# Graph network on one core: padding edges get rows of their own behind the slots, and the scatter to the slots carries no bound

## The reference

```
h_proj = jnp.einsum('nd,rde->rne', h, relation_weight)      # 32 relations, 64 x 64 each
t_r = h_proj[etype, src]
h_r = h_proj[etype, dst]
att = jnp.sum(t_r * jnp.tanh(h_r + efeat), axis=-1)         # one number for each edge
att_exp = jnp.exp(att - seg_max[dst])                        # softmax over the edges of a destination
a = att_exp / denom[dst]
h_nb = jax.ops.segment_sum(h[src] * a[:, None], dst, num_segments=N)
out = leaky_relu((h + h_nb) @ res_w1.T) + leaky_relu(h * h_nb @ res_w2.T)
```

## Time and profile before

| | before |
|---|---|
| median of 3 runs | 4424.13 us |
| lowest, highest | 4401.28, 4436.07 us |
| span of the profiled execution | 4246.6 us, instructions 40658 |
| PE / PEld / DVE busy | 49% / 39% / 64% |
| ACT / POOL busy | 33% / 68% |
| DMA | 547.79 MB, mean 129 GB/s |
| granted TensorE clock, mean | 0.657 of full speed |

### The profile page before, as it was taken

The page is one execution under the profiler, slowest core; times in us unless marked ns, Lnnn a source line. Parts: engine busy times, 40 slices in busy tenths (PEclk is TensorE's granted clock), DMA queues, the critical chain, the costliest instruction groups (busy, mean ns, idle before and its releaser), DMA issues.

```text
span 4246.6 us, 40658 instructions
## 1 busy us (share of the span) xinstructions
PE 2075.1 (49%) x10767; PEld 1665.6 (39%) x10767; DVE 2732.3 (64%) x5225; ACT 1412.2 (33%) x2876; POOL 2876.9 (68%) x4049
## 2 busy tenths in 40 slices
PE   6729995565664222122200004543556787676563
PEld 2216663444443121121100003443545666665563
DVE  9947765888886899999933324673776445444442
ACT  0028873332332222222210002211212211887773
POOL 8878867888885888676067776666666400578787
PEclk9969996555555555555555557776776766666665
DMA  6668864444443555555332224324334411122121
GB/s 236 240 234 262 262 233 142 131 133 142 142 140 123 158 171 170 181 171 166 118 78 76 67 69 140 112 59 127 110 96 122 127 56 48 50 67 56 55 57 29
DMA packets 261685, 547.79 MB, mean 129 GB/s; under 512 B 107792, under 2 KB 119930, under 8 KB 261462
## 3 DMA queue, kind: packets, MB, share of 16 engines
q1 hardware_dynamic: 179702, 445.68, 32.1%
q0 software_dynamic: 81760, 99.52, 9.7%
HBM read 275.18 MB, written 273.83 MB: 129 GB/s over the span
## 4 chain that ended last, share of the span: by engine, by line
POOL 50%; issue 19%; DVE 13%; PE 11%; ACT 4%; DMA 3%; POOLq 0%; SPq 0%; DVEq 0%; ACTq 0%
POOL arena L1316 17%; POOL work L1316 14%; POOL result L1311 8%; POOL slot_rows L1311 8%; POOL pause L1324 3%; PE banks L1887 2%; PE banks L1767 2%; PE banks L1896 2%; DMA work<-slot_rows 2%; DVE arena L810 1%; DVE arena L818 1%; PE banks L1868 1%; DVE work L620 1%; DVE arena L614 1%; PE banks L1947 1%
## 5 line engine op out<-in xcount | busy, mean ns | idle before, releaser
L1311 POOL DMA_INDIRECT result<-work,outi x392 | 475.4, 1213 | 368.5 <-DVE work L1018 247.3
L1311 POOL DMA_INDIRECT slot_rows<-work,dsafe x392 | 390.5, 996 | 280.9 <-POOL pause L1329 184.6
L1316 POOL DMA_INDIRECT arena<-g_by_node_and_edge,m_idx x392 | 453.3, 1156 | 168.2 <-POOL pause L1324 105.7
L1316 POOL DMA_INDIRECT work<-in_x,dsafe x392 | 439.6, 1121 | 112.6 <-POOL pause L1324 104.9
L1316 POOL DMA_INDIRECT arena<-h_by_node_and_edge,m_idx x392 | 412.6, 1053 | 111.5 <-POOL pause L1324 59.9
L1759 PE MATMUL banks<-ident,work 128*128 128x128 f32 x392 | 100.5, 407 | 718.9 <-ACT arena L1468 646.2
L1316 POOL DMA_INDIRECT arena<-input_and_place_by_node,src_i x252 | 313.1, 1243 | 74.6 <-POOL pause L1324 73.7
L1759 PEld LDWEIGHTS banks<-ident,work 128*128 128x128 f32 x392 | 68.9, 213 | 742.4 <-issue 662.2
L1854 PE MATMUL banks<-ident,work 128*128 128x128 f32 x556 | 118.0, 353 | 347.2 <-DMA work<-slot_rows 278.5
L1887 PE MATMUL banks<-pos,ident 112*128 112x128 f32 (+3 forms) x784 | 191.7, 385 | 79.1 <-DVE spare L909 58.0
L1958 PE MATMUL banks<-work,ident 128*128 128x65 f32 x784 | 170.8, 413 | 118.9 <-ACT work L1683 118.9
(11 more groups left out here) (332 smaller groups left out, 6861.2 us busy)
## 6 DMA issues: line engine op xcount, KB each, us to landing
slot_rows<-work SPq DMA_DIRECT2D x64, 834.0 KB, 7.9
work<-slot_rows SPq DMA_DIRECT2D x139, 384.0 KB, 3.4
input_and_place_by_node<-arena SPq DMA_DIRECT2D x49, 528.0 KB, 3.0
g_by_node_and_edge<-arena SPq DMA_DIRECT2D x49, 512.0 KB
arena<-x_of_destination SPq DMA_DIRECT2D x56, 448.0 KB, 4.2
work<-g_by_node_and_edge SPq DMA_DIRECT2D x49, 512.0 KB, 4.4
h_by_node_and_edge<-work SPq DMA_DIRECT2D x49, 512.0 KB, 6.6
work<-h_by_node_and_edge SPq DMA_DIRECT2D x56, 448.0 KB, 4.0
```

Source lines behind the costliest of these rows:

```text
L1311: pool.indirect_dma_start(out=table[:, :], out_offset=bass.IndirectOffsetOnAxis(ap=idx, axis=0), in_=of, in_offset=None, bounds_check=boun ...
L1316: pool.indirect_dma_start(out=to, out_offset=None, in_=table[:, :], in_offset=bass.IndirectOffsetOnAxis(ap=idx, axis=0)).then_inc(signal, 16)
```

## The change

`slot_rows` gets KE = 392 more rows behind the 71,168 slots. `slots_found` has one more instruction per part, which takes the smaller of the row number and `P * KS + column`. For an edge that is the row number it had; for a padding edge it is a row behind the slots, one for each column. The reads of `slot_rows` and its zeroing are limited to the first 71,168 rows. The scatter to the slots no longer passes a bound. In the built program the bound is a register, which a register move sets ahead of every scatter; these 392 moves are gone, 396 are left for the other scatters. Where a scatter is paced, the wait for the pause stood on the register move, and it now stands on the DMA itself. The scatter of results keeps its bound.

```diff
-        slot_t = nc.dram_tensor("slot_rows", (P * KS, RW), F32).ap()
+        slot_t = nc.dram_tensor("slot_rows", (P * KS + KE, RW), F32).ap()
...
-                os.did(ts(slot_row[:, lo:hi], slot_row[:, lo:hi], float(t0), None, ALU.add))
+                os.do(ts(slot_row[:, lo:hi], slot_row[:, lo:hi], float(t0), None, ALU.add))
+                os.did(stt(out=slot_row[:, lo:hi], in0=tile_no[:, 0:hi - lo], scalar=float(P * KS + lo), in1=slot_row[:, lo:hi],
+                           op0=ALU.add, op1=ALU.min))
...
-            lanes = slot_t.rearrange("(l s) w -> l (s w)", l=P)
+            lanes = slot_t[0:P * KS, :].rearrange("(l s) w -> l (s w)", l=P)
...
-            slots = slot_t.rearrange("(l s) w -> l s w", l=P)
+            slots = slot_t[0:P * KS, :].rearrange("(l s) w -> l s w", l=P)
...
+            def scatter_all(table, idx, of, signal):
+                pool.indirect_dma_start(out=table[:, :], out_offset=bass.IndirectOffsetOnAxis(ap=idx, axis=0),
+                                        in_=of, in_offset=None).then_inc(signal, 16)
+
...
-            def scatter_slowly(table, idx, of, bound, signal):
-                scatter(table, idx, of, bound, signal)
+            def scatter_slowly(table, idx, of, signal):
+                scatter_all(table, idx, of, signal)
...
-                    (scatter_slowly if s > PART_STEPS[1] else scatter)(slot_t, slot_row[:, t:t + 1], perm[:, q, k, :],
-                                                                       P * KS - 1, c_sent[q])
+                    (scatter_slowly if s > PART_STEPS[1] else scatter_all)(slot_t, slot_row[:, t:t + 1], perm[:, q, k, :],
+                                                                           c_sent[q])
```

## The result

The changed kernel takes 4662.47 us (median of 4, 4640 to 4663) against 4430.1 us of the kernel before (median of 4, 4401 to 4448): ratio 1.0525, interval 1.0478 to 1.0572. Predicted were 4337 us, faster. It is slower by some 232 us.

A forecast was written before the change was run, and what follows sets the result against it. POOL alone was taken to bound the kernel from 2180 to about 3178 us, the scoring chain behind that. 102 + 4 - 12 - 6 - 1 = 87 us off the median 4424 gave 4337 us, range 4295 to about 4390.

The forecast's parts named there:

- Paced scatters, 1.88 to 1.36 us: POOL's slot scatters, steps 9 to 27: 0.52 us saved each, 102 us for the 196 of steps 9 to 22.
- rival 3: Paced scatters: the 0.78 us idle belongs to the scatter, not the register move; 4420 us, chance 0.10.
- Unpaced scatters, 4 us: 126 slot scatters of steps 0 to 8: 0.03 us saved each, 4 us, if the bound takes the difference.
- New transfers and new DVE work, nothing: 176 padding rows written: nothing; five more DVE instructions: 1.5 us, of which 1 us counts.
- Given back to the scoring, 18 us: POOL waits for scoring on DVE, which falls behind: 12 us in part 0, 6 in part 1.
- the 102 of the first term: Saving on POOL from 196 paced scatters of steps 9 to 22, at 0.52 us each: 102 us.
- waits for ACT of some 12 us in steps 13 to 15: Expected sign: POOL waits some 12 us for ACT's copy of the scan there, less in steps 18 to 20.
- Rival 1: Scoring is less stiff than assumed and nothing is given back to it; 4318 us, chance 0.15.
- What lies around the span isn't touched.: Profiled span 4246.6 to about 4160 us; the same microseconds taken off the median, 4424 to 4337.
- Rival 4: Slower: busier POOL holds up DVE's small scoring instructions, 7 us per step for 1%; 4468 us, chance 0.04.
- Rival 2: Scoring steps stretch by 2.4 us each as slot loads take longer; gain 44, 4380 us, chance 0.16.
- The tail: From the last scan to 3608 us: as long as before, some 240 us.

The follow-up runs named there:

- e9: Kernel before with its bound in one register set once, so no move ahead of each slot scatter: 4657.27 us, ratio 1.0541.
- e18: Kernel before, bound in a register set once, two pauses behind first-stage gathers and scatters and gathers of steps 9 to 27: 4302.89 us, 0.9745.
- e17: Kernel before, bound and moves kept, with two pauses behind gathers of the first stage and of steps 9 to 27: 4369.26 us, 0.9914.
- e2: Kernel before with only the longer table, its 392 more rows never written or read: 4424.97 us.
- e4: Changed kernel with longer table and padding rows, but a bound and its register move again on the slot scatter: 4434.72 us.
- e1_before_again: Kernel before, unchanged, profiled once more: 4439.72 us, profile span 4479.8 us.
- e15: Changed kernel with two pauses behind first-stage gathers and behind scatters and gathers of steps 9 to 27: 4318.62 us, 0.9721.

## Why the prediction was wrong

*Paced scatters, 1.88 to 1.36 us.* Right: 1.37, with 0.28 of idle. The reading of the move was right, and rival 3 fell. e9 shows it from the other side: with the bound kept and the moves gone, the scatters stand 1.38 us apart. e18 against e17 shows what such a saving is worth where nothing is late: 66 us for 0.35 us per scatter.

*Unpaced scatters, 4 us.* About right: steps 0 to 8 last 354.5 instead of 355.3 us.

*New transfers and new DVE work, nothing.* Right (e2, e4).

*Given back to the scoring, 18 us.* This is the step that failed. I took what DVE needs, 184 us for four steps, as a property of the scoring alone, and let POOL's steps shrink against it. The need depends on POOL's pace: with the scatters at 1.37 us a step takes 62.9 us, not the 46 of that budget. The term was not 18 us but some 320: the 102 of the first term, all of it, and the 218 that the stage got longer. My waits for ACT of some 12 us in steps 13 to 15 are 24 to 30 us for each of the steps 11 to 15, and go on behind them. Rival 1, nothing given back, is off in the same direction.

*"What lies around the span isn't touched."* Wrong as a reading, and so is the sentence beside the table of times that the 155 to 190 us lie around the instructions. Span and time of the profiled execution are within 2 us of each other in every run behind the prediction; the profile ahead of the prediction was an execution in which PE's hand-overs were on time (2 + 6 us late in sum, none by over 1 us), and the timed runs were not like it. The profile could not warn of a delay that it did not contain. The gap of some 177 us between its span and the median could, and I explained it away. A second warning lay in the kernel: pauses behind DMAs, which do nothing for the result, keep DMAs apart, and a change that shortens the distance works against them.

*Rival 4* had the sign. It asked for 7 us more per scoring step to be slower by 1%, and it was 15 us and 5%, so its 4468 us is far too little. Its mechanism is not the one either. It asked for longer DVE instructions, and the exclusive lock of the Trainium skill (SBUF — State Buffer, on the shared pair) would show as such. The scans take 2158 ns on the mean in both kernels and the small ones of L886 and L884 424 and 421 ns. No row here shows POOL holding DVE: DVE was called late, and so was ACT. *Rival 2* named steps that stretch, by slot loads that take longer. A slot load takes 2.8 us from its issue to its last packet in both kernels (its packets of 3072 bytes 175 and 164 ns on the mean), and the share of the DMAs fell from 0.37 to 0.31. PE does wait more for slot loads, 252 against 153 us in the stretch, but a load itself takes no longer: SP issues it behind the DVE instruction that frees its buffer, and DVE is late. By this order of the program a late hand-over comes back to PE as a late load.

*The tail*, 240 us from the last scan on, was right: 3771.57 to 4009.93 = 238.

## What to carry to other kernels

An engine that is made faster off the arithmetic path can slow the others through how densely it issues, and a stray wait (here a register move behind a pause) may be the only thing that keeps it apart. Before taking such a wait away, measure it under a knob: one more pause here, one fewer there, on each kind of DMA, and keep the spacing while dropping the instruction. And compare the profiled span with the timed runs first: if they differ by 4%, the profile is of an execution that the timing does not see. All of this is from one kernel on one core, and from executions that were recorded; the last section says what that leaves open.

## What the runs showed of the hardware

Indirect DMAs that POOL issues 1.34 and 1.37 us apart go with late hand-overs from TensorE to ScalarE and VectorE, by up to 16.3 us in the changed kernel (287 us over 95 groups), while VectorE to ScalarE stays at 0.03 us. With gathers 1.49 and scatters 1.53 us apart there is next to none (12 us); no run here has both kinds at a spacing between. Both kinds count, gathers of 128 rows of 256 bytes and scatters of 768. The transfers did not queue up: the last packet of a step's scatters comes 1.0 us behind the end of the last scatter instruction in most steps and 2.5 us at most, in the changed kernel as before (2.0 at most).

What is late, PE's completion or its signal, I can't say. The Trainium skill (Perfetto Trace Analysis, on the per-instruction lifecycle) says that the end shown for a TensorE instruction is estimated, and that its semaphore is pushed when PSUM has acknowledged; the rows can't contradict it, and both readings fit. The trace's own record of the semaphore's change stands at the late time (3.49 us behind the products that end at 2817.28, which DVE takes 3.58 us behind), so that it is not DVE that is slow to see it. Nor is it settled why the execution shown first has none of it, with gathers 1.34 us apart too. It has 63,086 records of semaphore changes, e1_before_again, the same program, 36,718 and the changed kernel 35,926, so records are missing in the later ones. Their number alone does not go with the time: e15 has 39,525 at 4319 us, and e2 has 35,758 at 4425 us, as few as e9 (35,787) at 4657. Every timed run behind the prediction has a span and a granted clock on record, so each of them was recorded in some form. Whether the recording has a part in the delay, or both follow from something else, no run here tells apart, and so it is not shown that an execution without any recording loses time by the change.
